# When two quantisation chains of a fused attention and FP4 feed-forward kernel do their steps: later slots on VectorE, and one Wo product a slot later

## The reference

```
x = x + (softmax(q k^T / 8) v) Wo + bo          # q, k, v from layernorm(x)
x = x + fp4_linear(silu(gate) * up, w_down)     # gate, up = fp4_linear(layernorm(x), w)

def fp4_quant_dequant(x):                       # blocks of 16 along the last dimension
    scale = max(max(|xb|) / 6, 1e-12)
    q = GRID[searchsorted(MID, |xb / scale|)] * sign(xb) * scale
```

## Time and profile before

| | |
|---|---|
| median of the runs | 1429.57 us |
| the profiled execution: time, span | 1427.8 us, 1425.9 us |
| busy share of the span: PE, POOL, ACT, DVE | 94%, 80%, 80%, 77% |
| granted clock over the span | 0.981 |
| L475 POOL p_low, 1024 times | 1074 ns each |
| L781 ACT exponential, 1024 times | 772 ns each |
| L960 DVE maximum, 512 times | 1214 ns each, 207.5 us idle before them |

### The profile page before, as it was taken

One profiled execution on the slowest core, in us unless ns is written; L12 is line 12 of the kernel. 1 busy time (PEld: TensorE's weight loads), 2 busy tenths in 40 slices (PEclk: granted clock), 3 DMA queues, 4 the chain that ended last, 5 costly groups with the idle time before them and its releaser, 6 DMA issues.

```text
span 1425.9 us, 43020 instructions
## 1 busy us (share of the span) xinstructions
PE 1342.6 (94%) x17924; PEld 880.3 (62%) x17924; DVE 1092.8 (77%) x1719; ACT 1134.4 (80%) x2285; POOL 1143.3 (80%) x1135
## 2 busy tenths in 40 slices
PE   3899999999999999999999999999999999999965
PEld 2466666666666666666666666666666666666644
DVE  7767677677778778787877878787787878868577
ACT  2698887978888888888888888888888888888842
POOL 5688988878888888888888888878888887878832
PEclk8899999999999999999999999999999999999988
DMA  7122111121211112122111221211121221112000
GB/s 179 46 46 47 46 32 34 29 46 47 47 46 41 33 26 49 46 47 50 34 40 24 50 46 46 51 26 41 32 50 46 47 50 25 39 35 50 2 5 15
DMA packets 46687, 60.26 MB, mean 42 GB/s; under 512 B 8672, under 2 KB 21920, under 8 KB 46496
## 3 DMA queue, kind: packets, MB, share of 16 engines
q1 hardware_dynamic: 46336, 57.26, 17.1%
q10 hardware_dynamic: 160, 0.26, 0.1%
HBM read 4.80 MB, written 2.10 MB: 5 GB/s over the span
## 4 chain that ended last, share of the span: by engine, by line
PE 70%; DVE 20%; ACT 6%; issue 2%; DMA 1%; POOL 1%; SPq 0%; DVEq 0%
PE st L628 13%; PE st L630 11%; PE sm L610 8%; DVE negm L960 7%; PE ob L650 7%; PE ob L657 6%; PE ob L655 6%; ACT probs L781 4%; PE sm L548 2%; PE sm L1259 2%; PE mb L564 2%; PE sm L564 2%; DVE qv L1114 2%; PE mb L548 2%; PE sm L553 2%
## 5 line engine op out<-in xcount | busy, mean ns | idle before, releaser
L475 POOL TENSOR_TENSOR p_low<-probs 128x512 f16<-128x512 f32 x1024 | 1080.1, 1074 | 221.4 <-ACT probs L781 203.9
L781 ACT ACTIVATE probs<-st,lift,exp_scale 128x512 f32<-128x512 f32 x1024 | 775.1, 772 | 165.1 <-PE st L630 157.2
L960 DVE TENSOR_REDUCE negm<-sm 128x1 f32<-128x1024 f32 x512 | 616.0, 1214 | 207.5 <-PE sm L610 207.4
L628 PE MATMUL st<-q_hl,k_hh 128*128 128x512 f16 x1024 | 392.3, 383 | 6.8 <-ACT probs L781 6.7
L630 PE MATMUL st<-q_hm,k_l 128*128 128x512 f16 x1024 | 389.3, 380 | 0.0
L655 PEld LDWEIGHTS ob<-v,probs 128*128 128x128 bf16 x4096 | 289.6, 99 | 60.9 <-ACT o_raw L750 1.1
L655 PE MATMUL ob<-v,probs 128*128 128x65 f16 x4096 | 319.2, 193 | 0.7 <-ACT o_raw L750 0.7
L657 PE MATMUL ob<-v,probs 128*128 128x64 f16 x4096 | 319.7, 194 | 0.0
L657 PEld LDWEIGHTS ob<-v,probs 128*128 128x128 bf16 x4096 | 270.5, 97 | 59.9
L650 PEld LDWEIGHTS ob<-v,p_low 128*128 128x128 f16 x4096 | 177.8, 98 | 91.1 <-issue 1.6
L628 PEld LDWEIGHTS st<-q_hl,k_hh 128*128 128x128 f16 x1024 | 99.5, 97 | 154.7 <-issue 80.8
(11 more groups left out here) (205 smaller groups left out, 1612.7 us busy)
## 6 DMA issues: line engine op xcount, KB each, us to landing
k_hh<-k_high SPq DMA_DIRECT2D x128, 128.0 KB, 2.3
k_l<-k_low SPq DMA_DIRECT2D x64, 128.0 KB, 2.4
q_hl<-q_high SPq DMA_DIRECT2D x64, 128.0 KB, 2.3
q_hl<-q_low SPq DMA_DIRECT2D x64, 128.0 KB, 2.4
q_hm<-q_high SPq DMA_DIRECT2D x62, 128.0 KB, 2.3
x<-x SPq DMA_DIRECT2D x4, 512.0 KB, 7.2
q_hm<-m_high SPq DMA_DIRECT2D x128, 1.0 KB
q_hm<-m_low SPq DMA_DIRECT2D x128, 1.0 KB
```

Of the source, the lines that this page charges most:

```text
L475: return pool.tensor_tensor(p_low[b][:, j, :], p, p.bitcast(BF16)[:, 1::2], ALU.subtract)
L628: pe.matmul(st[s % 2][:, :], k_hh[n][:, s * P:(s + 1) * P], q_hl[n][:, half * HALF:(half + 1) * HALF], start=True, stop=False)
L781: nc.scalar.activation(probs[k % 2][:, s, :], st[s % 2][:, :], ACT.Exp, bias=lift[:, 0:1], scale=exp_scale[:, head, pair:pair + 1]).then_i ...
L960: nc.vector.tensor_reduce(negm[k % 2][:, pair % 4:pair % 4 + 1], banks.rearrange("p a n -> p (a n)"), AX.X, ALU.max, negate=True).then_inc ...
```

## The change

It edits the hand-written slots, no operation. In x's chain, parts 1 and 2 go from slots (3,2) and (3,3) of the odd round to (3,6) and (3,7); the lift goes from (3,5) of the odd round to (0,1) of the even one; part 3 goes from (3,6) of the odd round to (0,2) of the even one, part 4 from (0,2) to (0,3); part 5 stays at (0,6). In h's chain, in the odd round, part 1 goes from (0,2) to (0,3), part 2 from (0,3) to (0,6), the lift from (0,5) to (0,7), part 3 from (0,6) to (1,0); parts 4 and 5 stay at (1,2) and (1,3). In every round o0 goes from PE slot (1,5) to (1,6), behind t1, and its addition on DVE from (1,6) to (1,7).

```
-        ("o0", X0, (1, 5), None, (1, 6)), ("t1", X1, (1, 5), (1, 6), None), ("h0", MB, (1, 6), (1, 7), None),
+        ("t1", X1, (1, 5), (1, 6), None), ("o0", X0, (1, 6), None, (1, 7)), ("h0", MB, (1, 6), (1, 7), None),
...
-AT_X, AT_X_END = ((2, 7), (3, 2), (3, 3), (3, 6)), ((0, 2), (0, 6))
-AT_H_BEGIN, AT_H = ((3, 6),), ((0, 2), (0, 3), (0, 6), (1, 2), (1, 3))
+AT_X, AT_X_END = ((2, 7), (3, 6), (3, 7)), ((0, 2), (0, 3), (0, 6))
+AT_H_BEGIN, AT_H = ((3, 6),), ((0, 3), (0, 6), (1, 0), (1, 2), (1, 3))
...
-AT_X_LIFT, AT_H_LIFT = (3, 5), (0, 5)
+AT_X_LIFT, AT_H_LIFT = (0, 1), (0, 7)
...
-        n = ffn_two(r, 0)
+        n = ffn_two(r, 1)
         if n is not None and here == AT_X_LIFT:
             self.lift_steps(act, 2 * DIM, self.steps(n, False))
...
-                    self.quant(dve, self.small, self.xq[:, :], 2 * DIM, self.steps(n, False), part + 4)
+                    self.quant(dve, self.small, self.xq[:, :], 2 * DIM, self.steps(n, False), part + 3)
```

## The result

The changed kernel takes 1495.52 us (median of 4 runs, 1493.65 to 1498.22) against 1428.95 for the kernel before; the ratio is 1.0465, interval 1.045 to 1.048. The profiled execution took 1498.22 us, its span is 1496.4: 70.5 more than before. It is the slowest of the four, with a granted clock of 0.971 against 0.974 to 0.976 for the others; between the medians the difference is 66.6. Slower was right; the forecast of 1468 was 27 us too low, and the range ended at 1490.

The account below looks back on a forecast made before the run. PE, 94% busy, bounds the kernel: a round is its work plus its waits. Terms 23.1 - 9.6 + 14.3 + 6.5 + 3.0 + 1.0 = 38.3 on 1427.8 give 1466.1, median 1468; own range 1455 to 1481, wider 1443 to 1490.

Parts of the forecast that it names:

- the even start: Start of even rounds 10 to 30: x's parts 1 and 2 delay the first maximum, k0 waits about 1.3; +14.3 us.
- the odd end: End of odd rounds 9 to 31: the maximum of (3,4) starts earlier, 0.8 gained in each of 12; -9.6 us.
- o_n's 0.43: Wo product: t1, now in front of o0, waits for ACT's o_n, 0.43 late in 15 rounds; +6.5 us.
- Rounds 2, 4 and 6: Wo product: t1 waited even behind o0, so o0's time, about 1.0, is lost whole in each; +3.0 us.
- the first half of the odd rounds: Odd rounds 11 to 31: h's later steps delay the maxima and t1 by 2.1 us in each of 11; +23.1 us.
- Part 3 of h ... now comes here: 0.80: DVE in odd rounds: part 3 now precedes the second maximum, 0.80 long, making that maximum 2.1 us late.
- the work is the same (875.93 to 879.52), so these are 2.1 late too: Odd rounds, DVE: unchanged work from the second maximum to the maxima of (1,4) and (1,5), so 2.1 us late.
- The bound of 4.2: Upper bound per odd round in the h term, if two moved steps stand through a whole p_low, 1.07 each.
- the lock rule: DVE and POOL share ports under an exclusive lock: a moved step costs up to one p_low more where POOL issues first.
- Rival (2): The granted clock falls behind a longer wait once per odd round, 1.75 us each, 11 times: 19 us, 1487; chance 0.08.
- the two rivals: One: POOL ahead at moved steps, 21 us over 11 pairs, 1489, chance 0.17; other: the clock falls, 1487, chance 0.08.
- rounds 5 and 8: o0's addition stands behind three parts of the weights' quantisation, next scores wait: 0 to 1.2 us each, +1.0 for both.

Follow-up runs that it names:

- x alone: The kernel before with only the slots of x's chain changed (parts, lift); 1434.13 us, ratio 1.0041.
- the filled kernel: The changed kernel plus eight matmuls nobody reads, ahead of t1 in the odd rounds that quantise h; 1486.06 us, ratio 1.0404.
- POOL out of the way: The changed kernel with p_low cut to 8 of 512 columns in slots (0,6) to (1,3) of odd rounds quantising h; 1462.38 us, ratio 1.0237.
- the lift later: The changed kernel with ACT's lift of h at (1,2), parts 3 and 4 at (1,2), part 5 at (1,3); 1496.62 us, ratio 1.0474.
- The three parts alone: The kernel before with one part of the change each: the Wo product 1446.41 us, x's chain 1434.13, h's chain 1482.48.
- h alone: The kernel before with only the slots of h's chain changed (parts 1, 2, 3 and lift); 1482.48 us, ratio 1.0375.
- the addition earlier: The changed kernel with DVE's addition of o0 at (1,6) instead of (1,7); 1497.4 us, ratio 1.0479.

## Why the prediction was right and wrong

**Right: the even start and the odd end.** +14.3 with o_n's 0.43 in each of 11 rounds makes 19.0; measured 20.2. The wait at k0 was put at 1.3 and is 1.15, with L1110 free and L1119 held as assumed. The odd end was put at -0.8; with x alone it is -0.9, and round 9 of the changed kernel shows -0.37 against -0.8 + 0.43. Rounds 2, 4 and 6 gave 2.7 for 3.0. Every place named for a wait had one; a wait of 0.26 before the plain scores at (1,3) had not been named.

**Wrong in size: the first half of the odd rounds.** The step that failed is "Part 3 of h ... now comes here: 0.80", and behind it "the work is the same (875.93 to 879.52), so these are 2.1 late too". Both took durations as they stood, at a place where POOL has p_low queued back to back. Held parts 3 and 4 take 0.66 and 0.71 more than 0.88, 1.4 together. Counted from the first scores of rounds 21 before and 19 after (863.20 and 814.10), `m_low` comes 1.06 late where 1.3 was forecast, the second maximum behind part 3 2.54 late where it was 2.1, and the maximum behind parts 4 and 5, and t1 with it, 3.24 late where it was 2.1. Up to `m_low` the chain was priced well; the two held parts are the rest. The bound of 4.2, for two steps that stand through a p_low, took this in; the sum and the range did not use it. A round without a fall is 44.66 - 42.28 = 2.38 longer, where 2.1 - 0.8 = 1.3 was forecast: 11 x 1.08 = 12 us missing. The trace before had the warning: part 5, which follows part 4 directly, took 1.61 there for work that takes 0.89 with POOL short. From DVE's timeline of round 21, before:

```profile
877.98 1.61 DVE L1136 TENSOR_TENSOR hidden<-qv,q_small 128x704 f32<-128x704 f32 x1
```

By the lock rule of the Trainium skill weighed in the prediction (SBUF — State Buffer, "Who interferes with whom"), the pair of ports that the two engines share is an exclusive lock, and issue order decides which of them blocks. The runs agree: with a p_low ahead by 0.2 us parts 3 and 4 took 1.54 and 1.59, with p_low short 0.87. Of part 3, 0.74 was left when that p_low had ended, a little less than the 0.87 that it takes alone, so nearly all of it stood. The mistake was to weigh it only at the two steps that I knew to be moved next to a p_low, and not at every step whose start changes.

**Wrong in chance: the clock.** Rival (2), put at 0.08 because "the longest wait I expect is 1.5", followed once the wait was 2.19: six falls of 46.29 - 44.66 = 1.63 us, 9.8 in all, and the filled kernel gave back 9.5. The price (1.75 each) was close; its condition hung on the term above, so the two rivals were not separate cases: the first brings the second, and with POOL out of the way both are gone.

**Wrong in size: rounds 5 and 8.** "Between 0 and 1.2 each, +1.0 for both" is 7.2. Two things are in it. The addition does not wait for three parts' time on a free DVE; the parts are held by p_low too, and the scores behind the addition wait 3.21 us in round 5 and 1.91 in round 8. And the clock falls behind these waits, which the term left out: 6.8 us at the lower clock in round 5 instead of 3.4 before, and 3.4 in round 8 instead of none. Two other runs, POOL out of the way and the lift later, have the code of the changed kernel in both rounds, and their executions had fewer falls. These are the windows of round 5 in the two, in that order:

```profile
199.70:245.60 45.90, 40.17 (x550) 25.73 (x549) 35.40 (x62) 33.99 (x67) 35.23 (x37) 0.96 0.16 36
201.80:246.40 44.60, 38.84 (x549) 25.46 (x547) 35.36 (x62) 33.62 (x67) 35.11 (x37) 1.00 0.16 37
```

PE idles 5.7 to 5.8 us in each, as in the changed kernel, but the round takes 47.32, 45.86 or 44.60 with 6.8, 3.4 or 0 us at the lower clock. Round 8 takes 41.88 in both, without a fall. With as many falls as before, then, the rounds are 2.9 and 1.2 longer: 4.1 of the 7.2 are the waits, the other 3.1 two falls more. Round 7 went the other way: it had a fall before (42.42) and none in the changed kernel's execution (42.60), and in those two runs, with one, it takes 43.05.

12 + 9.8 + 6.2 + 1.2 is 29 of the 32 us between the sum of 38.3 and the measured 70.5. The remaining 3 are the start and the end of the execution, which no run took apart. They may be no effect of the change: the first scores start between 44.4 and 46.8 us in the profiles of all these kernels, and the changed kernel's are the latest.

The three parts alone cost 18.2, 5.9 and 54.2 us over the 1428.26 of their comparison, 78 together, and 67 in one kernel. Four more falls with h alone account for 6.5 of that; the rest was not followed up.

## What to carry to other kernels

Price a moved step on VectorE by what GpSimd does at its new place, not by its duration at the old one, and do so for all steps whose start moves, not only for those that are listed in the change. Put a step that nothing waits for behind the maximum that TensorE waits for, not ahead of it: the same two quantisation chains cost 60 us in one set of slots (5.9 and 54.2, each alone) and gained 17 in another. When a wait of TensorE comes near the length behind which the profile already shows a lower clock, add the fall to its price.

## What was not expected of the hardware

- Falls of the clock depend on more than the wait just before them: behind a wait of 2.19 to 2.20 us before t1 or o0 the granted clock went to 0.50 for 3.4 us in six of eleven odd rounds of the changed kernel, in seven with the addition earlier and in ten with h alone, behind 2.73 in eleven of eleven, and in the rounds behind up to 1.17 never. In round 5 the same waits, up to 3.21 us, had two falls, one or none. In round 8 a wait of 1.91 had one in the changed kernel and none with the lift later, so the "under 2" of that run's expectation is no limit. What decides was not settled.
- Eight matmuls of 512 columns that nobody reads made a kernel 9.5 us faster.
- L1119 on the same 704 elements took 0.51 here and 0.70 before; on 256 elements 0.28, 1.01 and 1.02.
